# First wide attention: even units turned by DMA transposes, second half of the queries by a repeated projection, later weights loaded between the transposes

## The reference

```
def _L0_xattn_ref(xq, xk, xv, mask, w_q, w_k, w_v, w_o, b_o):
    ...
    q = jnp.einsum('bsd,hdk->bhsk', xq, w_q)
    kk = jnp.einsum('btd,hdk->bhtk', xk, w_k)
    v = jnp.einsum('btd,hdv->bhtv', xv, w_v)
    scores = jnp.einsum('bhsk,bhtk->bhst', q, kk) / jnp.float32(d_k)
    masked = scores * mask[:, None, None, :]
    scores = jnp.where(masked == 0.0, -jnp.inf, masked)
    attn = jax.nn.softmax(scores, axis=-1)
    out = jnp.einsum('bhst,bhtv->bhsv', attn, v)
    ...
    return concat @ w_o + b_o
...
x = x + _L0_xattn_ref(_layernorm(x, axis=-1), ctx_1024, ctx_1024, mask_BxS2_ff1, L0_xattn_w_q, L0_xattn_w_k, L0_xattn_w_v, L0_xattn_w_o, L0_xattn_b_o)
```

## Time and profile before

| | |
|---|---|
| median of 3 runs | 524.99 us (524.94 to 526.46) |
| the profiled execution | 526.76 us, of which 525.0 us are its span |
| busy in the span | PE 485.2, PEld 276.2, DVE 428.9, ACT 328.1, POOL 266.7 us |
| L0x, scores to the last low half | about 25 to 139 us |
| granted TensorE clock, mean | 0.995 of 2.4 GHz |

### The profile page before, as it was taken

One profiled execution on the slowest core, in us unless ns is written; L12 is line 12 of the kernel. 1 busy time (PEld: TensorE's weight loads), 2 busy tenths in 40 slices (PEclk: granted clock), 3 DMA queues, 4 the chain that ended last, 5 costly groups with the idle time before them and its releaser, 6 DMA issues.

```text
span 525.0 us, 13065 instructions
## 1 busy us (share of the span) xinstructions
PE 485.2 (92%) x4770; PEld 276.2 (53%) x4778; DVE 428.9 (82%) x1209; ACT 328.1 (62%) x661; POOL 266.7 (51%) x294
## 2 busy tenths in 40 slices
PE   8889999999999899998899889997999999999996
PEld 4346555666864223334333456763555556954574
DVE  6999999999777778854786789987898989687663
ACT  4688888888436356663476387764778878323222
POOL 7957888777761924420014273415877778100200
PEclk9999999999999999999999999999999999999999
DMA  8552000000140000000000222001545445500000
GB/s 219 150 146 64 1 1 4 1 2 4 41 160 1 0 2 1 2 2 1 0 3 1 81 61 82 21 1 21 102 88 97 101 84 102 141 1 1 1 1 21
DMA packets 57875, 23.80 MB, mean 45 GB/s; under 512 B 41875, under 2 KB 56022, under 8 KB 57686
## 3 DMA queue, kind: packets, MB, share of 16 engines
q1 hardware_dynamic: 57814, 22.99, 18.0%
HBM read 14.33 MB, written 0.26 MB: 28 GB/s over the span
## 4 chain that ended last, share of the span: by engine, by line
PE 53%; DVE 20%; issue 15%; ACT 8%; POOL 3%; DVEq 0%; POOLq 0%; ACTq 0%
PE psM L502 5%; PE pspair L551 5%; PE psS L536 4%; PE psO L568 4%; ACT PP L1442 4%; PE psO L805 3%; PE pspair L780 3%; PE pspair L1085 3%; PE psS L395 2%; PE pspair L536 2%; DVE nmx L1974 2%; DVE Qst L1863 2%; DVE Zt L1850 2%; PE psS L754 2%; PE psS L1057 1%
## 5 line engine op out<-in xcount | busy, mean ns | idle before, releaser
L568 PE MATMUL psO<-V,PP 128*128 128x64 f16 x1536 | 60.8, 193 | 2.2 <-DVE Oall L1892 1.8
L1533 ACT ACTIVATE PP<-pspair 128x1024 f32<-128x1024 f32 x48 | 46.5, 1021 | 25.7 <-PE pspair L791 25.5
L551 PE MATMUL pspair<-ident,PP 128*128 128x128 f32 x384 | 61.6, 283 | 1.0 <-ACT PP L1442 0.9
L568 PEld LDWEIGHTS psO<-V,PP 128*128 128x128 f16 x1536 | 56.7, 98 | 6.5 <-DVE PP L1857 2.4
L551 PEld LDWEIGHTS pspair<-ident,PP 128*128 128x128 f32 x384 | 40.5, 140 | 28.0 <-issue 19.5
L2570 POOL TENSOR_TENSOR ln_rs<-ln_ve,minus_half 128x4 f32<-128x4 f32 x10 | 10.3, 1032 | 83.2 <-DVE ln_ve L1747 80.0
L1442 ACT ACTIVATE PP<-scores_m,nm 128x512 f32<-128x512 f32 x64 | 46.5, 727 | 5.4 <-DVE nm L1841 5.4
L1857 DVE TENSOR_TENSOR PP<-pspair,PP 128x512 f16<-128x512 f32 x65 | 44.4, 684 | 4.0 <-ACT PP L1422 4.0
L1422 ACT CAST PP<-pspair 128x512 f16<-128x512 f32 x65 | 37.9, 583 | 1.5 <-PE psO L568 1.1
L395 PE MATMUL pspair<-ident 128*128 128x512 f16 x134 | 33.9, 379 | 0.0
L502 PE MATMUL psM<-ctxTm,mask_i 128*128 128x512 f16 x96 | 26.1, 381 | 4.0 <-DVE Qst L1863 3.0
(11 more groups left out here) (618 smaller groups left out, 1294.1 us busy)
## 6 DMA issues: line engine op xcount, KB each, us to landing
W<-in_L_ffn_W SPq DMA_DIRECT2D x16, 256.0 KB, 3.0
bigw<-in_L_xattn_w_q SPq DMA_DIRECT2D x2, 512.0 KB, 7.1
bigw<-in_L_xattn_w_kv SPq DMA_DIRECT2D x1, 1024.0 KB, 4.8
V<-in_ctx SPq DMA_DIRECT2D x1, 512.0 KB, 4.2
bigw<-in_L_xattn_w_v SPq DMA_DIRECT2D x1, 512.0 KB, 5.7
mask_b<-in_mask_BxS_ff SPq DMA_DIRECT2D x1, 512.0 KB, 8.0
bigw<-in_L_xattn_w_k SPq DMA_DIRECT2D x1, 512.0 KB, 6.6
bigw<-in_L_xattn_w_o SPq DMA_DIRECT2D x1, 512.0 KB, 4.2
```

Source lines behind the costliest of these rows:

```text
L551: mm = pe.transpose(bank[b][:, k * P:(k + 1) * P], Pb[j % 4][:, k * P:(k + 1) * P], ident[:])
L568: mm = pe.matmul(bank["O"][:, (j % UPH) * a.dv:(j % UPH + 1) * a.dv], (PTH, PTL)[ppart][j % 4][:, k * P:(k + 1) * P], (VH, VL)[vpart][:, b ...
L1533: nc.scalar.activation(PX[k % 4], pairs[k % 2][:], ACT.Exp, scale=a.scale).then_inc(sem(f"{n}.exp"), 1)
```

## The change

In L0x the even units are no longer turned by PE. As in L2x, POOL halves the unturned exponentials (into acc and y_sb as two staging buffers, `stages` = 2, of L2x's four), and a DMA transpose turns them; `lag` is 4. Odd units are turned by PE and halved by ACT and DVE, as the even ones were. POOL's `split` is gone, and so is DVE's `query_low`: the low half of the queries is now a fifth projection, "Qrest", the three matmuls again and a fourth with `minus_dh` (minus 64 times the unit matrix) on the high half, taken out by ACT. K1 and the halving of its keys come one unit later. SP issues the loads from `mask_in` on in small groups, one behind each transpose (`later_loads`), and the routed matrices after the last transpose. `mask_prep` waits for the last two transposes, since it overwrites their staging buffers.

```
-        self.lag = 4 if self.by_dma else 3
-        self.per = 4 if mask else 3
+        self.lag = 4
+        self.stages = 2 if mask else 4
+        self.per = 5 if mask else 3
...
+                if what == "Qrest":
+                    mm = pe.matmul(bank["M"][:], minus_dh, Qst[k][:, 0:TOK], start=False, stop=True)
...
-                    turn(i, j)
+                    if j % 2:
+                        turn(i, j)
                     if not (first and j < a.lag):
                         values(*shift(i, j - a.lag))
...
+                    if j % UPP == 3 and more:
+                        project("Qrest", *following)
-                    if j % UPP == 4 and more and not (a.made and first and j < UPP):
+                    if j % UPP == 5 and more:
                         project("K1", *following)
...
+            def query_rest(i, k):
+                filled(act, f"{n}.proj", a.nth(PPI * i + k, "Qrest"))
+                nc.scalar.mul(Qst[k][:, TOK:2 * TOK], bank["M"][:], a.scale).then_inc(free["M"], 1)
...
-                dve.wait_ge(sem("L0x.split"), L0X.units // 2 - 1)
+                for d in (L0X.units // 2 - 2, L0X.units // 2 - 1):
+                    dma_done(dve, L0X, d)
...
-                        if j % UPP == 4 and more:
-                            query_low(*pair(i, j // UPP + 1))
...
-                        if own_low(a, i, j):
-                            evac(i, j)
+                        if j % 2 == 0 and not (first and j == 0):
+                            evac(*shift(i, j - 1))
...
+                    if a.mask:
+                        pool.wait_ge(sem(f"{n}.exp"), i * UPI + j + 1)
+                    else:
+                        emptied(pool, f"{n}.S{j % 4}", affine(i, j, UPI, 4))
+                    if d >= a.stages:
+                        dma_done(pool, a, d - a.stages)
...
-                        sp.dma_start_transpose(out=PTD[j % 4], in_=PS[d % 4])\
-                            .then_inc(sem(f"{a.name}.turned{d % 2}"), 16)
+                        sp.dma_start_transpose(out=PTD[j % 4], in_=PS[d % a.stages])\
+                            .then_inc(sem(f"wide.turned{d % 2}"), 16)
+                        if then is not None:
+                            then(d)
...
+            def later_loads(d):
+                if d == 0:
+                    sp.dma_start(mask_in[:], A["mask_SxS2_bk0"].rearrange("(q p) s -> p q s", p=P))\
+                        .then_inc(sem("ld.mask_in"), 16)
+                    sp.dma_start(bigw[:, 3, :].rearrange("p (c d) -> p c d", c=NPAIR),
+                                 A["L0_xattn_w_o"].rearrange("(c p) d -> p c d", p=P)).then_inc(sem("ld.L0wo"), 16)
+                elif d < 8:
+                    for name, n in ROWS[2 * (d - 1):2 * d]:
...
+                elif d < 29:
+                    expert_W1(d - 27, d - 27)
+                elif d < 31:
+                    expert_W2(d - 29, d - 29)
+
+            sp_turns(L0X, later_loads)
             filled(sp, "L0.V15")
```

More of the change, by code:

```diff
@@ L78, in nth @@
     def nth(self, pair_no, what):
-        m = {"K0": 0, "rest": 1, "Q": self.per - 2, "K1": self.per - 1}[what]
+        m = (("K0", "rest", "Q", "Qrest", "K1") if self.mask else ("K0", "Q", "K1")).index(what)
         return self.per * (pair_no - 1) + m - (self.made if pair_no > 1 else self.made // 2)
@@ L501, in project @@
                     for part, (wpart, cpart) in enumerate(PARTS):
-                        mm = pe.matmul(bank["M"][:], (wq16 if what == "Q" else wk16)[:, wpart, cols_],
-                                       X16[:, cpart, :] if what == "Q" else ctxTm16[:, cpart, keys],
-                                       start=(part == 0), stop=(part == 2 and what != "rest"))
+                        mm = pe.matmul(bank["M"][:], (wq16 if what in ("Q", "Qrest") else wk16)[:, wpart, cols_],
+                                       X16[:, cpart, :] if what in ("Q", "Qrest") else ctxTm16[:, cpart, keys],
+                                       start=(part == 0), stop=(part == 2 and what not in ("rest", "Qrest")))
                 else:
@@ L519, in pair_scores @@
                     elif b == 0:
-                        emptied(pe, f"{n}.proj", a.nth(PPI * i + k, "Q"))
+                        emptied(pe, f"{n}.proj", a.nth(PPI * i + k, "Qrest" if a.mask else "Q"))
                         if a.made and PPI * i + k == 1:
@@ L573, in values @@
                     mm.then_inc(full["O"], 1)
[L574 to L575 removed]
+                else:
+                    mm.then_inc(sem("wide.pv"), 1)
             def out_turn(c):
@@ L607, in rounds @@
                     following = pair(i, j // UPP + 1)
-                    if j % UPP == 0 and more and a.mask:
+                    if j % UPP == 0 and more:
                         project("rest", *following)
@@ L654, in pe_attention @@
                 emptied(pe, v)
-            run(pe, a, rounds_by_dma if a.by_dma else rounds)
+            run(pe, a, rounds if a.mask else rounds_by_dma)
             nr = a.units // UPI
@@ L1515, in act_attention @@
                 exps(0, 1)
-            run(act, a, rounds_by_dma if a.by_dma else rounds)
+            run(act, a, rounds if a.mask else rounds_by_dma)
         def act_packed(act, a):
@@ L1915, in rounds @@
                             recip(*group)
-                        if own_low(a, i, j):
-                            evac(i, j)
+                        if j % 4 == 3 and not (first and j < UPH):
+                            norm(*group)
+                        if j % 2 == 0 and not (first and j == 0):
+                            evac(*shift(i, j - 1))
                         if last and out_chunk(j) in a.dve_turns:
                             copy(f"{n}.oT{out_chunk(j)}", OT[out_chunk(j)])
+                    if last:
+                        evac(i, UPI - 1)
                 def rounds_by_dma(i, first, last):
@@ L1956, in attention @@
                         stat(0, j)
-                run(dve, a, rounds_by_dma if a.by_dma else rounds)
+                run(dve, a, rounds if a.mask else rounds_by_dma)
                 group = (a.units // UPI - 1, GPI - 1)
@@ L2614, in rounds @@
                 def rounds(i, first, last):
-                    for j in range(1, UPI, 2):
-                        if not own_low(a, i, j):
-                            split(i, j)
-                        if j % UPP == 5 and a.mask and not (last and j >= UPP):
+                    for j in range(0, UPI, 2):
+                        split_unturned(i, j)
+                        if j % UPP == 6 and not (last and j >= UPP):
                             split_keys(*pair(i, j // UPP + 1))
-                run(pool, a, rounds_by_dma if a.by_dma else rounds)
+                run(pool, a, rounds if a.mask else rounds_by_dma)
             def spreads(a, meanwhile=None):
@@ L2788, in _, with sp_turns @@
         def _(sp):
-            def sp_turns(a):
+            def sp_turns(a, then=None):
                 def rounds(i, first, last):
```

142 lines of the change are left out of this document (67 added, 75 removed).

## The result

The changed kernel takes 533.06 us (median of 4 runs, 531.94 to 534.14) against 525.73 for the kernel before beside it: ratio 1.0139, 95% interval 1.0108 to 1.0169. It is 7.3 us slower, where 6 us faster was forecast. Its profiled execution took 531.94 us, with a span of 530.2 and a mean granted clock of 0.996.

What follows compares the result with a forecast made beforehand. DVE was taken to pace L0x's pairs of 13.76 us, PE close behind. DVE's work -6.1, chain waits +1.0, loads +0.5 and L0x's end -1.5 gave -6.1 us: 518.9 us, range 516.8 to 523.5.

Steps and rivals of the forecast that it cites:

- ACT's part: L0x pairs: chain through ACT and psM, 7.6 us against DVE's 7.7; waits 0 to 0.5 a pair, 1.0 us lost in all.
- DVE's part: L0x pairs: without query_low 12.97 us instead of 13.76; with 0.60 in the eighth pair 6.1 us gained, if nothing else interferes.
- PE's part: L0x pairs: four turns go, Qrest comes in, PE's round falls 0.9 us; less PE work alone is worth only 0.18.
- POOL and the transposes: L0x: transposes land in 3.1 us, at the longest 4.8; in the steady part nothing of them is on the path.
- The rival that a loop of POOL and DMA makes it slower: L0x pairs: two staging buffers make halvings wait for transposes; a pair could take 14.2 us, time 528; chance 10 in 100.
- The loads: Between L0x's transposes: two 512 KB loads delay the next transpose in the queue, 0 to 1.8 us for both, 0.5 taken.
- The end of L0x: Last maximum to last norm: mask_prep starts earlier and runs faster beside idle POOL; 2.9 us gained to 1.1 lost, 1.5 gain taken.
- that the projection bank paces: L0x pairs: 0.5 us of waiting a pair instead of 0.15, 2.5 us less gain, 521.4 us; chance 18 in 100.
- rival 3: Start and end of L0x: loads cost 1.8, the end 1.1, the chain 0.5 a pair; 524 to 525.3 us; chance 10 in 100.

Runs made afterwards that it cites:

- e3: The changed kernel without the fifth projection Qrest, the low half of the queries again made on DVE: 532.22 us, ratio 1.0106 to the kernel before.
- e7: The changed kernel with PE's values of odd units three units behind instead of four, and norm ahead of the zeros: 522.69 us, ratio 0.9908.
- e11: e7 without Qrest, the low half of the queries again made on DVE: 525.67 us, ratio 0.9974 to the kernel before.
- e8: e7 with ACT's copy of K1 one unit earlier too: 521.36 us, ratio 0.9903 to the kernel before.
- e12: e7 with the loads of the first eight transposes issued ahead of the first transpose: 521.01 us, ratio 0.9877 to the kernel before.
- e6: The changed kernel with ACT's copy of K1 one unit earlier, ahead of the odd unit's cast: 529.67 us, ratio 1.0028 to the kernel before.
- e10: e7 with the loads of transposes 8 to 30 issued behind the last transpose and the routed matrices: 527.08 us, ratio 1.0009.

## Why the prediction was wrong

**The step that failed** is "ACT's part", with the bounds of 0 to 0.5 us a pair for waits, and the words "if nothing else gets in DVE's way". Waits cost 14.74 - 12.97 = 1.77 us a pair. The chain there ran from a maximum to scores by way of ACT and psM and came to 7.6 us against DVE's 7.7. In the changed kernel's trace it takes 8.9 us, from the end of unit 4's maximum (62.09) to the end of the scores behind K0 (70.95); DVE's own work between the two is 7.8, and DVE stands the 1.10 us that are left. The chain left out psO: the change also moves `norm` behind the two `zeros` (1.2 us later in its round) and gives the units turned on PE the longer lag too. It took `values` as 0.35 us of work, where in the trace the first `values` of a group stand for `norm`, 0.32 us at 65.06 and 0.86 at 72.75, each cast of an odd unit stands for `values`, and DVE's `zeros` then stand for the scores behind them. It also left out ACT's copy of Qrest (65.06 to 65.64), for which the scores at 65.70 stand; e3, without Qrest, still takes 14.61, so that is not the main part. I compared busy time and one chain; the loop through psO was in the order of both engines, but I didn't follow it. The mended order (e7) gives back nearly all of the 1.77. (The "half-pair rounds" of 3.24 us in the prediction are rounds of two units, a quarter of a pair; the sum is right.)

**DVE's part** was right in size: with the loop open a pair takes 13.02, not 12.97, DVE is full, and Qrest is worth 0.56 (forecast 0.61). Of the 0.60 in the eighth pair the change got 0.17, and e7 0.79. **PE's part** was right: 0.81 less a pair (0.9), and less PE work alone is worth the 0.18 that the prediction gave it: e11, in which DVE has the work of the kernel before, takes 13.58 instead of 13.76. **POOL and the transposes** were right: a median of 3.1 us, and the slowest, 5.7, lay in the first pair. The rival that a loop of POOL and DMA makes it slower had the right sign and the wrong mechanism: POOL waited for a DMA 5.2 us in all of L0x in three times, once from 50.5 to 125 us, and the pairs were alike to the hundredth. Only in the mended order do transposes lengthen single pairs (e8, e12).

**The loads**: 0.5 forecast, bounds 0 to 1.8. In the change they don't show, as its first pair takes 14.74 like the others; in the mended order they cost 14.51 - 13.02 = 1.5 us. (2 us less 1.2 of slack is 0.8 for each load, so the bound was 1.6 and not 1.8; the 1.5 lies within either.) The Trainium skill (DMA: Bandwidth & Descriptors, section Queues, rings and completion order) has descriptors of a queue consumed in ring order on each engine; e7 beside e12 agrees, since with the same transposes only the loads ahead of them moved, and the median out of acc went from 4.2 to 3.1 us. Loads that shared the DMA engines with the transposes without any order would delay them too, so no run here shows the order itself.

**The end of L0x**: -0.89 instead of -1.5. `mask_prep` went at 0.43 us as said, the transpose landed later than said (issued 3.7 us after the last maximum's end, landing 3.1: +6.9 us instead of +5.8), and the last `norm` then stood 1.07 us for `values`, a step that the forecast doesn't have: `mask_prep` alone would have let it go at +8.5. The halving of the routed matrices was covered, as forecast: POOL is done with it at 153.15, and PE first uses them at 156.97. But POOL's memsets stand behind it and so fall on the layer norm of L0f, where DVE's ln_ve takes 1.39 us; from the additions to X to the first product of L0f 7.21 us became 7.76. DVE's timeline of the kernel before has for it

```profile
148.54 0.17 DVE L1747 TENSOR_SCALAR ln_ve<-ln_mv 128x4 f32<-128x4 f32 x1
```

**The rivals**: that the projection bank paces was half right: its sign came true (DVE stood 1.10 us for the scores behind K0), K0 stood 0.9 us a pair, and e6 got 0.60 of it back, but that wait was one link of the loop, and once `norm` and the lag were mended its worth could not be told (e8). Start and end (rival 3) gave nothing back: the loss lies in the pairs.

## What to carry to other kernels

Where engines run fixed orders that hand buffers to each other, busy time bounds the period only from below: for each buffer with a single copy (here psO and psM) follow who empties it and what stands ahead of the emptying instruction, until the chain comes back to where it began, and compare that length with the busiest engine's round. A loop with two links that wait for each other gives nothing, or a loss, when one is mended, so try both before the idea is dropped. Keep a longer lag to the work that needs it, and put large loads where the DMA engines stand idle.

## What was unexpected of the hardware

DVE's ln_ve, 4 elements a partition, took 1.39 us in the changed kernel and 1.71 in e7, each time until about the end of POOL's memsets that ran beside it (0.95, 0.33 and 0.36 us, the first from 153.09), against 0.17 before, with POOL at rest. The other traces fit: wherever it starts, ln_ve ends 0.02 to 0.03 us behind the last of these memsets (1.92 us in e8, 1.49 in e10, 0.53 in e11), and in e12, where they end 0.23 us before it starts, it takes 0.17, with POOL's casts of 0.29 us beside it. `mask_prep` gives the same picture: 1.26 us an instruction beside POOL, 0.43 with POOL at rest. The Trainium skill (Trainium Architecture — The Big Picture, section What this means for kernel authors) calls the port pair that DVE and GpSimd share an exclusive lock, not a split of bandwidth; the small instruction that waits whole memsets out agrees; that the port is the reason, no run here shows.

The pairs of one kernel were equal to 0.01 us in the change (14.73 to 14.74), so a difference of 0.1 us between two orders could be read from one trace, where the medians of the runs scatter by some tenths of a per cent. That holds only while no transpose reaches the path: in e7, e8 and e12 the pairs of one kernel differ by 0.3 to 1.1 us.
